# Second mixture of experts: splitting each tile's row scaling between VectorE and GpSimd by columns

## What is computed

```python
scores = jax.nn.sigmoid(logits) * mask
masked_inputs = scores.T[:, :, None] * x[None, :, :]
gate_up = jnp.einsum('eth,ehf->etf', masked_inputs, gate_up_proj)
gate, up = jnp.split(gate_up, 2, axis=-1)
expert_out = jnp.einsum('etf,efh->eth', up * jax.nn.silu(gate), down_proj)
shared = jax.nn.silu(x @ w_gate.T) * (x @ w_up.T) @ w_down.T
out = shared + expert_out.sum(axis=0)
```

## Time and profile before

| | us |
|---|---|
| median of 3 runs | 833.33 (832.67 to 834.03) |
| the profiled execution | 833.27 |
| its span in the trace | 831.5 |
| TensorE busy in the span | 798.1 (96%) |
| VectorE busy | 606.1 (73%) |
| ScalarE busy | 555.5 (67%) |
| GpSimd busy | 493.1 (59%) |

### The profile page before, as it was taken

How to read it: one execution, slowest core, us unless ns; L and a number is a source line. 1 busy time by engine, 2 the same in 40 slices (tenths; PEclk the granted TensorE clock), 3 DMA queues, 4 the chain that set the end, 5 groups by cost and what they waited for, 6 DMA issues and landing times.

```text
span 831.5 us, 31624 instructions
## 1 busy us (share of the span) xinstructions
PE 798.1 (96%) x11875; PEld 698.3 (84%) x11875; DVE 606.1 (73%) x1741; ACT 555.5 (67%) x1221; POOL 493.1 (59%) x598
## 2 busy tenths in 40 slices
PE   8999998999899979999999999999999999989997
PEld 3666665666799969999999999999999999989997
DVE  7888888867466568987777777777778667645445
ACT  4898887665677767776666666666575755257662
POOL 6323443667345367876566767575766546548871
PEclk9999999999999999999999999999999999999999
DMA  6444665718344323332421111010101002523215
GB/s 156 136 125 132 211 201 157 195 59 311 109 130 141 110 78 117 117 91 85 158 85 56 29 33 38 25 38 25 38 25 34 16 18 88 107 68 81 73 38 203
DMA packets 86373, 81.84 MB, mean 98 GB/s; under 512 B 15489, under 2 KB 73416, under 8 KB 85458
## 3 DMA queue, kind: packets, MB, share of 16 engines
q1 hardware_dynamic: 76818, 64.27, 26.0%
q0 software_dynamic: 7744, 14.91, 6.0%
q10 hardware_dynamic: 1664, 0.64, 0.5%
HBM read 41.86 MB, written 36.16 MB: 94 GB/s over the span
## 4 chain that ended last, share of the span: by engine, by line
PE 82%; DVE 8%; issue 3%; DMA 2%; ACT 2%; POOL 2%; SPq 0%; ACTq 0%; POOLq 0%; DVEq 0%
PE of L1515 8%; PE sf L1469 8%; PE jf L1390 7%; PE sf L1431 4%; PE sf L1757 4%; PE mf L1417 4%; PE sf L1769 4%; PE jf L1399 4%; DVE cmx L2191 3%; PE sf L1399 3%; PE sf L1641 3%; PE sf L1657 3%; PE mf L1641 2%; PE of L1228 2%; PE sf L1181 2%
## 5 line engine op out<-in xcount | busy, mean ns | idle before, releaser
L1012 POOL TENSOR_TENSOR pl<-pT,ph 128x512 bf16<-128x512 f32 x128 | 146.2, 1166 | 100.2 <-DVE ph L2462 94.2
L2468 DVE TENSOR_REDUCE cmxb<-mf 128x8 bf16<-128x1024 f32 x64 | 78.2, 1221 | 40.7 <-PE mf L1496 40.7
L931 POOL DMA_INDIRECT buf<-gu,slots x64 | 64.1, 1001 | 64.1 <-PE of L1317 14.8
L1989 ACT ACTIVATE pT<-sf 128x1024 f32<-128x1024 f32 x64 | 66.7, 1042 | 23.3 <-PE sf L1479 23.3
L2191 DVE TENSOR_REDUCE cmx<-mf 128x8 bf16<-128x1024 f32 x64 | 78.1, 1220 | 5.1 <-PE mf L1209 3.9
L1001 POOL DMA_INDIRECT gb<-eo,slots x64 | 66.2, 1035 | 19.1 <-issue 18.2
L1469 PE MATMUL sf<-qTs,kTs 64*128 64x128 f32 x1024 | 74.4, 285 | 1.0 <-ACT pT L1989 1.0
L1871 ACT ACTIVATE pTf<-sf 128x1024 f32<-128x1024 f32 x64 | 62.6, 1020 | 11.6 <-PE sf L1188 11.1
L1469 PEld LDWEIGHTS sf<-qTs,kTs 64*128 64x128 f32 x1024 | 62.1, 187 | 6.4 <-issue 1.5
L1390 PE MATMUL jf<-late,oT 128*128 128x128 f32 x496 | 62.9, 280 | 0.0
L1121 POOL DMA_INDIRECT results<-rows x47 | 46.9, 997 | 18.7 <-issue 11.3
(11 more groups left out here) (375 smaller groups left out, 2710.7 us busy)
## 6 DMA issues: line engine op xcount, KB each, us to landing
buf<-zero SPq DMA_DIRECT2D x22, 256.0 KB, 3.9
eo<-zero SPq DMA_DIRECT2D x22, 256.0 KB
late<-in_ctxP SPq DMA_DIRECT2D x24, 192.0 KB, 2.9
rows<-buf SPq DMA_DIRECT2D x71, 64.0 KB, 2.0
gu<-in_gu SPq DMA_DIRECT2D x4, 1024.0 KB, 6.3
kept<-kTs SPq DMA_DIRECT2D x6, 512.0 KB, 3.8
kTs<-kept SPq DMA_DIRECT2D x6, 512.0 KB, 4.2
rows<-buf SPq DMA_DIRECT2D x47, 65.0 KB, 1.9
```

What stands on the lines that cost most here:

```text
L931: nc.gpsimd.indirect_dma_start(out=buf0[:, :], out_offset=bass.IndirectOffsetOnAxis(ap=slots0[:, k, b:b + 1], axis=0), in_=xna0[:, b, :], ...
L1012: nc.gpsimd.tensor_tensor(pl[h][:, :, c, :], pT[h][:, :, c, :], ph[h][:, :, c, :], ALU.subtract)\
L1989: nc.scalar.activation(pT[h][:, :, :, :].rearrange("p r c n -> p r (c n)"), S1, ACT.Exp, scale=D1 ** -0.5)\
L2468: nc.vector.reduce_max(cmx1[b % 2][:, :].rearrange("p (r k) -> p r k", r=2)[:, :, 4 * h:4 * h + 4], M1p[:, :, :].rearrange("p r (c k) -> p ...
```

## The change

Each tile is scaled by both engines: VectorE takes columns 0 to 63, GpSimd columns 64 to 127. TensorE waits for both counters before each transpose, and SyncE for both before it fetches again into a landing semaphore's turn. `scaled_at` lists all tiles instead of the even ones by the same formula, so that i = 12 has tile 0, i = 13 tiles 1 and 2, i = 14 tiles 3 and 4, and then one tile at each unit that is six before a tile. GpSimd scales its halves of tiles 0 to 10 ahead and then the half of tile n + 11 before the scatter of each tile n, up to n = 35.

```diff
-AHEAD, ODD_AHEAD = 6, 12
+AHEAD, POOL_AHEAD, HALF = 6, 11, DM // 2
...
-    return [t for t in range(0, TILES1, 2) if max(PLACE["tile", t] - AHEAD, FIRST_SCALE + (t + 1) // 2) == i]
+    return [t for t in range(TILES1) if max(PLACE["tile", t] - AHEAD, FIRST_SCALE + (t + 1) // 2) == i]
...
-                    need(sp, scaled[t % 2], (t - XSEMS) // 2 + 1)
+                    need(sp, scaled[0], t - XSEMS + 1)
+                    need(sp, scaled[1], t - XSEMS + 1)
...
-                    nc.gpsimd.tensor_scalar(xs1[t % XRING][:, 0:DM], xs1[t % XRING][:, 0:DM],
+                    nc.gpsimd.tensor_scalar(xs1[t % XRING][:, HALF:DM], xs1[t % XRING][:, HALF:DM],
                                             xs1[t % XRING][:, SCORE:SCORE + 1], None, ALU.mult).then_inc(scaled[1], 1)
 
-                for t in range(1, ODD_AHEAD, 2):
+                for t in range(POOL_AHEAD):
                     scale(t)
                 for n in range(TILES1):
-                    if n % 2 == 1 and n + ODD_AHEAD < TILES1:
-                        scale(n + ODD_AHEAD)
+                    if n + POOL_AHEAD < TILES1:
+                        scale(n + POOL_AHEAD)
...
-                    pe.wait_ge(scaled[t % 2], t // 2 + 1)
+                    pe.wait_ge(scaled[0], t + 1)
+                    pe.wait_ge(scaled[1], t + 1)
...
-                    nc.vector.tensor_scalar(xs1[t % XRING][:, 0:DM], xs1[t % XRING][:, 0:DM],
+                    nc.vector.tensor_scalar(xs1[t % XRING][:, 0:HALF], xs1[t % XRING][:, 0:HALF],
```

## The result

| | before | changed |
|---|---|---|
| median | 833.43 us (20 runs) | 837.35 us (20 runs, 833.62 to 840.31) |
| ratio, 95% interval | 1 | 1.0048 (1.0033 to 1.0063) |
| profiled execution, span | 833.27, 831.5 | 839.49, 837.7 |

An execution in a slower state, over 1.5% above the fastest of its kernel, is left out of every ratio and fit here; one of the 20 before is such (4348.77 us), and without it their median is 833.33. The changed kernel is slower by 3.9 us in the median; 837.0 was forecast, in a range from 834.4 to 840.6. The profiled execution lies 6.2 us over the one before, so it is not the median: it holds something that the forecast doesn't have, and the first rows show it. These are rows of the timeline of the changed kernel, at the start of the stage; they answer to the earlier trace rows.

What follows compares the result with a forecast made beforehand. TensorE was taken to set the pace from the first transpose on. A start loss of 1.3 us plus 2.45 us from the late last scatter, 3.75 us on 833.27, gave 837.0 us, in a range from 834.4 to 840.6.

Steps and rivals of the forecast that it cites:

- TensorE sets the pace, nothing to win: From the first transpose on TensorE is always busy; its only wait, 3.25 us, is for a fetch, hardly for the scaling.
- First tile, 0.23 us: At the start, the first transpose needs both halves, so TensorE's load moves from 730.80 to 731.03, 0.23 us later.
- Second tile, 1.29 us with the first: VectorE scales tile 1's left half behind unit 13's product, so TensorE loads 1.29 us later, the first tile's 0.23 included.
- S = 0.52: GpSimd's scaling of a 128x64 half by a per-row scalar takes 0.52 us, the middle of 0.42 and 0.62.
- The round, 1.73 us: One GpSimd half scaling plus one scatter takes 1.73 us, while tiles come every 1.56 us.
- The last scatter, 3.29 us late, 2.45 at the end: GpSimd's last scatter begins at 817.24 against 813.95; 0.84 us of the delay is spare, 2.45 reach the end.
- TensorE waits for GpSimd from S = 0.515: Near tile 46 GpSimd's half is level with the transpose at S = 0.52; TensorE loses 35 x (S - 0.515).
- The sum: Start loss 1.3 plus late last scatter 2.45 make 3.75 us on 833.27, giving 837.0 us.
- Pace kept: Rival: with S at or below 0.43 GpSimd keeps pace, only the start is lost, 834.6 us; chance 0.25.
- Hindrance: Rival: each of GpSimd's 35 rounds waits for one VectorE scaling, adding up to 8.8 us, to 845.8; chance 0.05.

Runs made afterwards that it cites:

- e3: Changed kernel, but VectorE scales its half of tile 1 at i = 12, right behind tile 0: 834.45 us, ratio 1.0021 to the kernel before.
- e1: Changed kernel, but from tile 11 on GpSimd takes one column and VectorE 127: 834.55 us, ratio 1.0014 to the kernel before.
- e2: Changed kernel, but from tile 11 on GpSimd takes 127 columns and VectorE one: 843.15 us, ratio 1.0123 to the kernel before.

## Why the prediction was right, point by point

- **TensorE sets the pace, nothing to win.** Held. No version was faster than the kernel before, and what moved the time was TensorE's start and the last scatter.
- **First tile, 0.23 us.** The load came 0.30 us later (2.49 behind the fetch against 2.19), 0.28 and 0.39 in e3 and e1.
- **Second tile, 1.29 us with the first.** The mechanism is shown by e3; the size was too small: 1.7 us in e1 (5.32 us behind the fetch against 3.60). I had moved the product of unit 13 by 0.23; it starts 4.49 us behind the fetch against 3.88, so 0.61 later: 0.39 from the first load, and 0.16 of idle time behind that transpose, which the forecast didn't have.
- **S = 0.52.** It is 0.457, nearer to the line through the 128x4 form (0.42) than I chose. I had held a slope above that of a two-input operation to be unlikely; the runs give 2.6 ns a column, and that two-input form has 1.94. The rule that gave 0.525 from 1.8 cycles an element (the Trainium skill, GPSIMD Engine Reference, section 3.1) is further off in its slope, 1.5 ns, and its S as far off as mine.
- **The round, 1.73 us.** It is 1.704: S is 0.06 shorter, and the gap between a scatter and the next scaling is 0.04 longer than in the earlier trace rows. 35 rounds took 59.64 us instead of 60.55. The gap of 0.01 was that behind the first scatter only; in later rounds of the kernel before it is already 0.03 to 0.04. With S = 0.457 and its own 1.21 us beside it the sum would have had rounds of 1.667 us, a last scatter 1.1 us late and 834.8 us in all, next to the rival in which GpSimd keeps pace. The S that was too long hid the fixed part that was too short. The scaling behind the scatter of 745.85, which ends at 746.82:

```profile
746.86 0.62 POOL L1110 TENSOR_SCALAR rows<-rows 128x128 f32<-128x128 f32 x1
```

- **The last scatter, 3.29 us late, 2.45 at the end.** From scatter 0 to the last it is 73.82 us against 71.34: 2.5 late, and 1.5 reach the end (e3: 1.6), where 2.5 less the 0.84 to spare is 1.6. e1 and e2 show that it is this term: it goes when the rounds are short, and grows one for one when they are long.
- **TensorE waits for GpSimd from S = 0.515.** At 0.457 it didn't; at 0.634 in e2 it did, by 2.2 us where 35 x (S - 0.515) gives 4.2.
- **The sum.** 1.3 + 2.45 was forecast; the traces give 1.7 + 1.5 at full clock. The two errors partly cancel. At equal clock the time says 2.4 (1.8 to 2.9), a little less than the traces' 3.2. Of the rest of the median's 3.9, 1.1 is the lower clock of its executions, a term that the forecast didn't have, and some 0.4 lies between medians and means (the means differ by 3.4). The closeness of 837.0 to 837.35 is thus in good part luck.
- **The rivals.** Pace kept: refuted on the first chip by the wait for the results; on the other two the time shows no loss clear of the scatter, and not because GpSimd kept pace: its 35 rounds took as long. Hindrance: VectorE's halves took 249 ns in the median and up to 518, GpSimd's 437 to 514, so both engines on each tile cost nothing to speak of in these durations, and before the change VectorE's longest was 529 as well. The rule of the Trainium skill (SBUF — State Buffer, Who interferes with whom) may be at work in the longest of VectorE's; its idle time covered them.

Whether the change itself makes the clock fall more often stays open. The mean clock was 0.0018 lower than the kernel before's on the first chip and 0.0016 on the others (0.9711 against 0.9727), some 2 and 1.6 times the standard error; yet e1, with the same start, had 0.9942.

## What to carry to other kernels

Splitting an operation over two engines halves only the part that grows with its width, and it gives the slower issuer twice as many instructions: price the fixed part, in the loop of the engine that has least time per round. Before moving work between engines, write down in which iteration each engine now does it and in which the consumer wants it, the first ones above all; here one place in a list cost 1.35 us in the traces, nearly as much as the 1.5 of the whole steady state. And find the slack of the last piece of each chain (0.84 us here), as it decides whether a slower pace shows at all.

## What the runs showed of the hardware

- A GpSimd multiplication by a per-row scalar costs 309, 457, 634 and 621 ns at 1, 64, 127 and 128 columns of float32, while an addition of two inputs takes 199 at 4 columns and 439 at 128. The one with a single tensor input is the dearer one.
- VectorE's scaling went from 280 to 249 ns when its width was halved, and took 204 at one column (e2): some 0.2 us is there whatever the width.
- The wait of TensorE at this place doesn't tell whether its clock falls: behind waits of 2.97 and 2.59 us the granted clock was 0.50, for 6.8 and 3.4 us, and behind waits of 3.25, 2.45 and 2.44 us it stayed at 1.00, one execution each. The falls went with a first scatter some 2.1 and 0.95 us later. Filling the wait with matmuls didn't raise the mean clock of the executions (0.9902 over six, against 0.9914).
- The same program takes 833 us on one chip and 875 to 878 on two others. In two traces from these, ScalarE is at times idle for 2 to 3 us (2.68 and 2.03 us) with its product already done; on the first chip, between 745 and 815 us, its waits end after 1.0 us at most.
